# One attention kernel, two ways to a softmax share: product on GpSimd against exponentials and inverse sums fed straight to ScalarE and VectorE

## The reference, cut to what matters

```python
def attention(hidden_q, kv_c, Wq, w_kc_q, w_kc_kv, W_qr, W_kr, Wo):   # B 32, S 128, 16 heads, R 64
    q_big = einsum('bshk,hkq->bshq', (hidden_q @ Wq.T), w_kc_q)
    kv_rope = kv_c * cos + rotate_half(kv_c) * sin
    q_r = einsum('bshq,hqr->bhsr', q_big, W_qr)
    k_r = einsum('bld,hdr->bhlr', kv_rope, W_kr)
    attn = softmax(einsum('bhsr,bhlr->bhsl', q_r, k_r), axis=-1)
    ctx_c = einsum('bhsl,bld->bhsd', attn, kv_rope)
    return einsum('bhsd,hkd->bshk', ctx_c, w_kc_kv).reshape(b, s, H * K) @ Wo.T

x = x + tanh(g_xattn) * attention(layernorm(x), ctx_512, ...)
x = x + tanh(g_ffn) * (moe_routed(layernorm(x)) + shared_mlp(layernorm(x)))   # 8 experts, top 2, capacity 1280
```

## Time and profile before

| | |
|---|---|
| median of 3 runs | 1944.63 us (1944.35 to 1944.76) |
| profiled execution, its own time | 1942.95 us |
| span of the trace | 1941.1 us |
| TensorE busy | 1863.6 us, 96% of the span |
| VectorE busy | 979.2 us, 50% |
| ScalarE busy | 665.6 us, 34% |
| GpSimd busy | 644.7 us, 33% |

### The profile page before, as it was taken

One profiled execution on the slowest core, in us unless ns is written; L12 is line 12 of the kernel. 1 busy time (PEld: TensorE's weight loads), 2 busy tenths in 40 slices (PEclk: granted clock), 3 DMA queues, 4 the chain that ended last, 5 costly groups with the idle time before them and its releaser, 6 DMA issues.

```text
span 1941.1 us, 32103 instructions
## 1 busy us (share of the span) xinstructions
PE 1863.6 (96%) x11801; PEld 1027.1 (53%) x11972; DVE 979.2 (50%) x1839; ACT 665.6 (34%) x1873; POOL 644.7 (33%) x683
## 2 busy tenths in 40 slices
PE   7799999999999998899999999999999999999999
PEld 7455655555555554344455555555544444444444
DVE  5777777777777777466332222222224423333233
ACT  4656566666666666220122222222110000000000
POOL 4645544455544566100223433343112101010101
PEclk9999999999999999999999999999999999999999
DMA  9446566666666767613289999989832522121202
GB/s 303 121 101 131 125 129 133 135 139 134 136 136 126 166 153 153 147 53 111 62 178 229 246 219 221 217 214 216 173 94 103 110 81 87 28 82 33 76 26 84
DMA packets 477332, 262.53 MB, mean 135 GB/s; under 512 B 410528, under 2 KB 416288, under 8 KB 477216
## 3 DMA queue, kind: packets, MB, share of 16 engines
q1 hardware_dynamic: 465696, 223.13, 49.9%
q0 software_dynamic: 11520, 37.76, 7.0%
HBM read 112.96 MB, written 48.23 MB: 83 GB/s over the span
## 4 chain that ended last, share of the span: by engine, by line
PE 70%; DVE 12%; ACT 8%; issue 5%; DMA 2%; SPq 1%; POOL 1%; DVEq 0%; ACTq 0%; POOLq 0%
PE score L738 12%; PE o L828 8%; PE score L817 7%; PE o L607 6%; PE p_bank L738 6%; PE m_bank L738 6%; PE o L750 5%; DVE arena L1022 5%; ACT arena L902 4%; PE p_bank L656 4%; PE p_bank L817 4%; PE m_bank L817 4%; PE c_bank L750 3%; PE t_bank L750 3%; DVE arena L1114 2%
## 5 line engine op out<-in xcount | busy, mean ns | idle before, releaser
L607 PE MATMUL o<-arena 128*128 128x512 bf16 x1474 | 339.1, 379 | 4.4 <-DVE arena L1022 1.2
L1022 DVE TENSOR_TENSOR arena<-arena 128x512 bf16<-128x512 f32 (+2 forms) x347 | 284.7, 826 | 20.4 <-ACT arena L924 4.9
L1412 POOL TENSOR_TENSOR arena<-arena 128x512 f32<-128x512 f32 x128 | 155.3, 1213 | 298.8 <-DVE arena L1043 298.8
L902 ACT ACTIVATE arena<-score,arena 128x128 f32<-128x128 f32 x512 | 181.8, 370 | 180.8 <-DVE arena L1114 180.8
L738 PE MATMUL score<-arena 128*128 128x512 bf16 x1035 | 234.0, 379 | 2.2 <-ACT arena L980 0.6
L607 PEld LDWEIGHTS o<-arena 128*128 128x128 bf16 x1536 | 147.8, 98 | 155.7 <-DVE arena L1022 1.1
L656 PE MATMUL p_bank<-arena 128*128 128x256 bf16 x1536 | 179.1, 273 | 0.8 <-DVE arena L1022 0.7
L738 PEld LDWEIGHTS score<-arena 128*128 128x128 bf16 x1056 | 103.2, 98 | 126.2 <-ACT arena L980 1.1
L1504 POOL TENSOR_TENSOR arena<-arena 128x1088 bf16<-128x1088 f32 x32 | 72.0, 2250 | 274.9 <-ACT arena L932 274.9
L828 PE MATMUL o<-arena 128*128 128x512 bf16 (+1 forms) x681 | 160.0, 379 | 2.0
L656 PEld LDWEIGHTS p_bank<-arena 128*128 128x128 bf16 x1536 | 145.3, 98 | 24.1 <-DVE arena L1022 1.0
(11 more groups left out here) (164 smaller groups left out, 2676.8 us busy)
## 6 DMA issues: line engine op xcount, KB each, us to landing
xrow_d<-arena SPq DMA_DIRECT2D x80, 256.0 KB
arena<-w_expert SPq DMA_DIRECT2D x32, 544.0 KB, 5.7
arena<-w_shared SPq DMA_DIRECT2D x22, 384.0 KB, 3.6
arena<-x SPq DMA_DIRECT2D x16, 512.0 KB, 4.6
arena<-x SPq DMA_DIRECT2D x32, 256.0 KB, 3.5
x_d<-arena SPq DMA_DIRECT2D x32, 256.0 KB, 2.5
xn_d<-arena SPq DMA_DIRECT2D x32, 256.0 KB, 2.4
arena<-x_d SPq DMA_DIRECT2D x8, 1024.0 KB
```

The source lines that it names most:

```text
L607: mm = pe.matmul(o_bank[b % 2][:, :], lhsT=cT[u % 2][:, a, h, :], rhs=M_w[:, w, head_of(hg, h), :], start=(hg == 0 and n == 0), stop=(hg = ...
L902: mm = act.activation(prob[:, u % 4, h, :], score_bank[u % 2][:, h * S:(h + 1) * S], ACT.Exp, bias=neg_max[:, u % 4, h:h + 1], accum_out=d ...
L1022: return dve.tensor_tensor(dst, src, hi, ALU.subtract)
L1412: pool.tensor_tensor(prob[:, u % 4], prob[:, u % 4], rden[:, u % 4, :].unsqueeze(2).broadcast_to([P, 4, S]), ALU.mult).then_inc(normed, 1)
```

## The change

The change has five parts.

1. GpSimd's product and the semaphore `normed` are gone. ScalarE makes the share's HI with four `activation(Copy, scale=rden)` of 128 columns and now waits for `inverted`. VectorE makes the share's LO with four `scalar_tensor_tensor` of 128 columns, `prob * rden - HI`.
2. In m = 2 ScalarE's `upper_piece` stands before the exponentials, and VectorE's two LO of the first layernorm stand behind the LO of the piece.
3. The rope operations on the rows move on GpSimd from m = 1 to m = 3.
4. `XS_STEP` goes from 118 to 121.
5. At the seam to the feed-forward part ScalarE's first two `silu_step` go between the last attention steps. On TensorE `down(0)` and the second half of `gate_up(2)` stand before the last two `route`, which now write to halves of `p_bank` and wait for `silu_done`; `down(1)` stands right behind them, and the last two `logits_of` wait for both routes.

```diff
@@ share HI on ScalarE
-                    wait(act, normed, u + 1, 16, it)
+                    wait(act, inverted, u + 1, 16, it)
                     wait(act, pT_in[(u - 2) % 4], 16 * ((u - 2) // 4 + 1), 64, it)
-                    act.copy(share[u % 2][:, HI, :], prob[:, u % 4].rearrange("p h n -> p (h n)"))\
-                        .then_inc(share_hi, 1)
+                    for h in range(4):
+                        mm = act.activation(share[u % 2][:, HI, h * S:(h + 1) * S], prob[:, u % 4, h, :], ACT.Copy,
+                                            scale=rden[:, u % 4, h:h + 1])
+                    mm.then_inc(share_hi, 1)
@@ ScalarE's order in m = 2
+                if m == 2:
+                    upper_piece(k + 12, it)
                 if k % 2 == 0:
                     exps(k + 6, it)
-                upper_piece(k + 12, it)
+                if m != 2:
+                    upper_piece(k + 12, it)
@@ share LO on VectorE
-                    lower(share[u % 2][:, LO, :], prob[:, u % 4].rearrange("p h n -> p (h n)"),
-                          share[u % 2][:, HI, :]).then_inc(share_lo, 1)
+                    for h in range(4):
+                        ins = dve.scalar_tensor_tensor(out=share[u % 2][:, LO, h * S:(h + 1) * S], in0=prob[:, u % 4, h, :],
+                                                       scalar=rden[:, u % 4, h:h + 1],
+                                                       in1=share[u % 2][:, HI, h * S:(h + 1) * S],
+                                                       op0=ALU.mult, op1=ALU.subtract)
+                    ins.then_inc(share_lo, 1)
@@ GpSimd
-                    wait(pool, inverted, u + 1, 16, it)
-                    pool.tensor_tensor(prob[:, u % 4], prob[:, u % 4],
-                                       rden[:, u % 4, :].unsqueeze(2).broadcast_to([P, 4, S]),
-                                       ALU.mult).then_inc(normed, 1)
...
-                if m == 1 and within((k + 7) // 8, NG):
-                    g = (k + 7) // 8
+                if m == 3 and within((k + 5) // 8, NG):
+                    g = (k + 5) // 8
@@ TensorE at the seam
             pe.wait_ge(x1_done, NB)
+            down(0, None)
+            gate_up(2, None, (1,))
+            pe.wait_ge(silu_done, 2)
             for b in (NB - 2, NB - 1):
-                route(b, o_bank[b % 2], None)
+                route(b, last_route(b), None)
+            down(1, None)
             pe.wait_ge(lg_up, NB)
-            down(0, None)
@@ logits_of on VectorE
-                wait(dve, lg_mm, b + 1, 4, it)
+                wait(dve, lg_mm, b + 1 if b < NB - 2 else NB, 4, it)
@@ ScalarE at the seam
-            run_steps(act, step)
+            run_steps(act, step, NU)
             silu_step(0, None)
+            for k in range(NU + 1, LAST_STEP - 1):
+                step(k, None)
             silu_step(1, None)
+            for k in range(LAST_STEP - 1, LAST_STEP + 1):
+                step(k, None)
```

More of the change, by code:

```diff
@@ L790, in _ @@
                     pe.wait_ge(slots_up, 1)
-                if v == 2:
-                    gate_up(2, None, (1,))
                 if v > 2:
                     gate_up(v, None)
-                if v not in (0, 1, 4, 14):
+                if v not in (0, 1, 2, 4, 14):
                     down(v - 1, None)
@@ L1081, in step @@
                           dst[:, HI, jp, :]).then_inc(pr_lo, 1)
+                if m == 2 and within(c + 2, NG):
+                    for s in range(2):
+                        wait(dve, xn1_hi, 2 * (c + 2) + s + 1, 4, it)
+                        lower(xn1_rows[s][:, LO, :], x_ln[:, s, :], xn1_rows[s][:, HI, :]).then_inc(xn1_lo, 1)
                 links(*((4, 5) if m == 0 else (7, 8, 9, 10, 11)))
```

15 lines of the change are left out of this document (5 added, 10 removed).

## The result

The changed kernel takes 1966.34 us (median of 4 runs, 1965.45 to 1967.46) against 1944.49 us before (1942.23 to 1944.76): ratio 1.0115, 95% interval 1.0098 to 1.0133. It is slower by 21.9 us, where +8.4 was forecast.

The account below looks back on a forecast made before the run. TensorE, busy 96.28 of 100 us, was taken to set the pace, with VectorE next. Terms -23.8 + 28 + 0.5 - 2 + 4.75 + 1.2 = +8.65 gave 1953 us; range 1928 to 1970.

Parts of the forecast that it names:

- rival (C): Attention loop: both rests and the rope meet in m = 6, stall 3.3 per period, about 1971 us; chance 0.15.
- Part 2, -23.8: Loop, m = 3: the earlier piece copy and later layernorm lowers remove TensorE's stall, 14 x 1.7 = -23.8 us.
- the new stall: Loop, mostly m = 0 and 1: VectorE's pieces come late, 2.0 per period, 14 x 2.0 = +28 us.
- the blocking: VectorE's share parts held up by GpSimd's rests and ropes in m = 4 to 7: together 5.7 us, before 2.3.
- the 35.9: VectorE's stretch from m = 2's piece to m = 0's, by steps with waits: 35.9 us, where TensorE allows 33.9.
- the 3.8: Part of VectorE's added work in that stretch absorbed by its idle time: 39.7 summed, 35.9 left, 3.8 us swallowed.
- the 0.50 case: Main case: GpSimd gets between VectorE's four share parts, new stall 2.0 per period; 1943 to 1963 us, chance 0.50.
- Rival (B): VectorE's share parts in m = 5 to 7 uninterrupted, or interrupted only once each: 1924.8 up to 1940 us; chance 0.27.
- Where shared weights are split as well (k from 98) GpSimd has more to interleave: +0.5: Late attention steps, k from 98: GpSimd's splits add operations to interleave with VectorE's parts, +0.5 us.
- The seam, +4.75 +1.2: Seam to feed-forward: last logits 4.75 us later, TensorE loses +4.75; new idles lower the clock, +1.2 us.
- Part 4, -2: Routers: moving four transposes on SP behind earlier load steps cuts TensorE's waits there, -2 us, bounds 0 and -3.3.
- running ahead: GpSimd, no longer held each step by its product, does both ropes in m = 6 and 7, interrupting VectorE there.

Follow-up runs that it names:

- Parts 2, 3, 4: The kernel before with the m = 2 order, row ropes in m = 3 and later transposes, old shares and old seam kept: 1921.46 us, ratio 0.9879.
- The order alone: The kernel before with only the order of step m = 2 changed on ScalarE and VectorE: 1932.25 us against 1944.83, ratio 0.9935.
- the kernels with small operations: The changed kernel with GpSimd's ropes and rests cut to 2 columns from step 16: 1928.74 us; with ropes already cut from the third group: 1927.58 us.
- the seam alone: The kernel before with only the seam's new order and ScalarE's early silus: 1950.28 us, ratio 1.0024.
- Paced: The changed kernel with GpSimd also waiting for the inverse sums in each step where its product stood, without any work: 1990.70 us, ratio 1.0237.

## Why the prediction was right and wrong

**Term by term.** Parts 2, 3, 4 give -23.4 (forecast -23.8 - 2), the new shares +41.7 (forecast +28 + 0.5) and the seam +3.2 (forecast +4.75 + 1.2). The mechanism and the direction were right; the term that was mis-sized is that of the new shares, by 13.2. The time is near rival (C)'s 1971, but not by its cause: TensorE's waits in the loop sum to 1.8 a group, not 3.3.

**Part 2, -23.8, was right in size and wrong in owner.** Parts 2, 3, 4 give -23.4. The order alone gives -12.6, because VectorE's moved lowers make the piece of m = 3 late for the scores of m = 4 (0.88). It is the ropes in m = 3 that take this second wait away; I had costed them inside part 1. By which step of VectorE's chain they do it isn't worked out, so that the sum of the two came to my number is in part luck.

**Part 1, the new stall: mechanism and place right.** I had put the blocking at 0.9, 1.8, 1.1 and 1.9 for m = 4 to 7. Over the 1.11 of four undisturbed parts the trace has 0.90, 1.82, 0.93 and 1.5. The waits stand at L662 and L658 of m = 7, 0 and 1, and sum to 1.8 where I had 2.0. That closeness is less sure than it looks: the 35.9 behind the 2.0 was not written out, so how the 3.8 was swallowed can't be compared. The parts themselves: 0.344 and 1.11 for four on VectorE, where I had 0.34 and 1.04; ScalarE's 0.42, which start about 0.29 apart, so 1.3, above my 1.1 and inside its bounds. The Trainium skill's page VectorE: DVE Perf Modes, section "The TRN2 errata — SBUF-src ops pay a fixed extra latency per instruction", would have given an estimate of 0.78 for the four; the measurement decides. Its advice against small operations held: four quiet parts take 1.11 where one `scalar_tensor_tensor` of 512 columns takes 0.74 in the same trace (L1074, at 369.04, with `o` for one operand). That GpSimd gets in at each opening was the 0.50 case, and it is shown: make GpSimd's operations small and 37.6 us go; make four of one lower and 73.7 come, some 22 of them through the clock. Rival (B), that the parts pass uninterrupted, is out.

**The step that failed is "Where shared weights are split as well (k from 98) GpSimd has more to interleave: +0.5".** The shares' 13.2 too many lie there and in the start-up. Between units 12 and 103 they cost 517.0 - 492.0 = 25.0, or 2.2 a group, near my 2.0. But between units 103 and 127, three groups, they cost 138.7 - 127.2 = 11.5, or 3.8 a group, where 3 x 2.0 + 0.5 = 6.5 was forecast. Timelines of VectorE and of GpSimd in the changed kernel, m = 3 of such a group:

```profile
711.79 2.46 DVE L1063 SCALAR_TENSOR_TENSOR arena<-arena 128x128 bf16<-128x128 f32 x4 [0.91 <-ACT arena L862]
...
715.43 0.68 DVE L1034 TENSOR_TENSOR arena<-p_bank,arena 128x512 bf16<-128x512 f32 x1
```

```profile
710.66 1.64 POOL L1486 TENSOR_TENSOR arena<-arena 128x768 bf16<-128x768 f32 x1 [9.46 <-ACT arena L932]
712.27 0.77 POOL L1467 TENSOR_TENSOR arena<-arena 128x256 f32<-128x256 f32 x1
713.12 0.46 POOL L1468 TENSOR_TENSOR arena<-arena 128x128 f32<-128x128 f32 x1
```

The ropes stand behind a split that waits 9.46 us for ScalarE, so they can't run ahead, and they meet the parts of m = 3, quiet in the loop. The parts take 2.46 there, the piece behind them is late, and TensorE waits at the scores:

```profile
693.16 2.79 PE L658 MATMUL p_bank<-arena 128*128 128x256 bf16 x24 [1.69 <-DVE arena L1034]
...
716.25 0.85 PE L636 MATMUL score<-arena 64*128 64x128 bf16 x24 [1.78 <-DVE arena L1034]
```

I had worked the chain of a loop group only and added a remainder for the others; these groups needed their own. With the ropes back in m = 1 these units still take 136.2, so the ropes' place explains 2.5 of the 11.5, and the rest is the other operations between the parts and what their waits bring, since with small ones 10.3 of it are gone. Some 1.7 of them, an estimate (half of the stretch), come from some 3 us at half clock, which parts 2, 3, 4 and the kernels with small operations don't have there (windows view):

```profile
775.00:777.00 2.00, 2.00 (x7) 0.75 (x8) 1.90 (x4) 1.06 (x3) 1.33 (x1) 0.64 0.81 178
```

It comes behind a wait of 2.79 that ends at 773.48.

**The start-up had no term at all.** Units 0 to 12 take 3.2 us more than before and 4.0 more than with parts 2, 3, 4. They take 63.8 to 65.3 in the six kernels with the new shares and full ropes there (64.4 on the mean), against 58.7 to 62.3 (60.9) in the eight with VectorE's share in one part. That the new shares cost some 3.5 there is shown by these. TensorE is at half clock for 3.4 to 10.2 us of this stretch in the six and for 0 to 4.0 in the eight, on the mean 6.3 against 2.2, so an estimate of up to 2 of the 3.5 is clock; by which wait it comes, and the rest, stays open.

**The seam, +4.75 +1.2, was close for the seam alone and too high on top of the other parts.** It costs 5.45 alone, 3.2 on parts 2, 3, 4, and 4.3 by the stretches. The logits were not as late as forecast: the last ones are added up 46.1 after the row maximum of unit 127, where it was 43.3 before, so 2.8 later and not 4.75. The two waits came where they were forecast, in the changed kernel's timeline:

```profile
845.55 1.47 PE L752 MATMUL o<-arena 128*128 128x512 bf16 x6 [2.36 <-DVE arena L1034]
...
854.66 2.74 PE L752 MATMUL o<-arena 128*128 128x512 bf16 x6 [5.49 <-DVE arena L1034]
```

and behind the second the granted clock was at 0.50, 1.2 GHz, for some 3 us (windows view):

```profile
855.00:857.00 2.00, 2.00 (x6) 0.76 (x5) 1.43 (x2) 1.98 (x2) 0.00 (x0) 0.50 0.48 134
857.00:859.00 2.00, 2.00 (x9) 0.84 (x8) 0.00 (x0) 1.97 (x5) 0.00 (x0) 0.88 0.74 217
```

That the logits' lateness is most of the price is shown by putting the routes first: 2.4 to 3.5 us go, and one wait of 0.9 stands in place of 7.8, with the new one of 3.8.

**Part 4, -2, was wrong:** nothing. **Part 3** was costed as part of running ahead, which I took for a harm. Paced, the kernel is 24.4 slower, some 8 of it through the clock.

By stretches, after against before: start-up and what is ahead of it +4.9 (forecast 0), units 12 to 103 +6.0 and units 103 to 127 +9.3 (together +15.3, forecast +2.7), the seam and behind +4.3 (forecast +5.95). Of the 15.3 the loop's 6.0 is +0.5 a group, where I had +0.3.

## What to carry to other kernels

Where VectorE reads two SBUF operands and GpSimd is busy, count instructions, not elements: in these traces each boundary between two VectorE instructions could let one whole GpSimd operation in, so work that is split into n parts can be held up n times. Taking an operation off GpSimd doesn't help if it leaves more boundaries on VectorE. And when a steady stall is costed, write the chain out again for every stretch where another engine's order differs (start-up, a phase with extra work); here 0.5 stood for 5.5. Look at TensorE's granted clock behind each new wait too: where the wait had grown to 2.1 us, many groups paid for a stretch at half clock besides.

## What the runs showed of the hardware

A 128-column `scalar_tensor_tensor` between SBUF operands is 0.344 us with GpSimd quiet, and each takes 1.24 to 1.27 when a 512-column GpSimd operation has got in ahead of it, so the wait is that operation's whole length (1.15 to 1.34) less an overlap. The page SBUF — State Buffer, section "SBUF: two separate sides", of the Trainium skill has the lock held for the whole instruction, and the trace agrees. What I had not expected is the size at one small change: the same subtraction in four instructions instead of one, with nothing else touched, made the whole program 3.8% slower, close to a third of it, by the estimate above, through the clock.
